# Jumping knowledge as one block: turned messages normed, weighed and summed in place in PSUM

## The chip, the cores and the metric

The kernel runs on one NeuronCore of a Trainium2 chip. The metric is the device time of one execution in microseconds, the median of several runs.

## The reference

The program is a chain of four graph networks over 50000 nodes with 128 features and 25000 edges, sorted by their end `dst`; each network's output is added to its input and the sum is layer-normed. The change is in the third network alone (jumping knowledge), which runs four layers:

```python
norm_src = rsqrt(max(deg_out, 1)); norm_dst = rsqrt(max(deg_in, 1))
for i in range(4):
    agg = segment_sum((h * norm_src)[src], dst, num_segments=n)
    h = relu((agg * norm_dst) @ Ws[i] + bs[i])
    mu, var = mean(h, axis=0), var(h, axis=0)
    h = relu((h - mu) * rsqrt(var + 1e-5) * gammas[i] + betas[i])
    xs.append(h)
out = relu(max(stack(xs), axis=0) @ lin1_w + lin1_b)
```

A node that no edge ends in has the same row in every layer, `relu(bs[i])` before the norm.

## The kernel before, in words

All sizes are fixed: the 25000 edges lie in 25088 slots, 49 groups (`EG`) of 512 (`GROUP`), each of four pieces (`SUB`) of 128. `K.goes_on` (a byte per slot) tells whether a slot has the same end as the one before it, `K.last_row` whether it is the last of its end, `K.l2_weight` holds each slot's weight, a number per partition. A layer's rows are stored to a table in HBM, `jk0` to `jk2`, one row per slot and one more row that all nodes without edges share; `idx_jk` points a slot at the row of its source, and at that shared row if the source is no edge's end. Layer 0 reads the table `x2` (in the trace `x`) instead.

`jk_start_block` makes the weights and the shared rows. Then `jk_layer_block` runs once for each layer, and each block opens and closes with a barrier of all engines. In a layer, each group goes through these steps:

- POOL (`pool_gather`, L570) issues four indirect DMAs, each of 128 rows, into `jk_layer_msg`, five groups deep (`DEEP`). It waits until the buffer's user of five groups ago is done.
- In layers 1 to 3 DVE puts the norm of the layer before on the rows: it multiplies by `W.jk_scale_row` (L1908) and adds `W.jk_shift_row` (L1910), into `jk_layer_ready`. These are rows, spread over the partitions at a layer's end by two matmuls.
- ACT weighs (`scalar_weigh`, L1023, four instructions a group, with Relu in layers 1 to 3), PE turns the rows into columns in PSUM (`tensor_sum`, L1057), DVE sums along the slots with a scan (L1079, PSUM to SBUF).
- PE multiplies by the layer's matrix (`make`, L696), ACT adds the bias and takes Relu (`keep`, L1886), SP stores the result turned (`jk_t`), DVE takes the two moments over the last slots of each end (`count`, L1916 and L1919, both with an accumulator).
- In layers 0 to 2 PE turns it back (`turn`, L687), ACT copies it out (L1891), and SP stores it to the table (L1850) from which the next layer gathers.

`run_groups(engine, n, stages)` writes an engine's program: it goes through the steps and calls each stage for the group that its lag says, so the order on an engine is fixed in the code. `g.lag(k)` is the group k before, and `wait_for` waits until that group has passed the named point. At a layer's end DVE works out scale and shift from the moments, with a root on ACT, and the barrier follows.

## Time and profile before

| | us |
|---|---|
| time, median of 3 runs (6713.34 to 6717.9) | 6714.33 |
| span of the profiled execution | 7555.6 |
| the four layers' gathers, first to last of each | 4005.5 to 4297.5, 4327.3 to 4623.0, 4653.4 to 4951, 4980 to 5268.5 |

No time beside its span is given for the profiled execution. It is 841 us or 12.5% above the median, so lengths in the trace are those of a slower execution than the timed ones. A busy time is that of an engine's own work; idle time before a group of instructions is named with what ended it, and "issue" is the engine's own pause between two instructions.

### The profile page before, as it was taken

What the parts mean: (1) busy time and instruction counts of PE and PEld (TensorE: products, weight loads), DVE (VectorE), ACT (ScalarE), POOL (GpSimd) and SP (SyncE); (2) the same over time, 40 slices, a digit from 0 to 9 for tenths busy, and PEclk for the clock granted to TensorE, in tenths of its full rate; (3) what the DMA queues carried; (4) which work ended last, traced back from release to release, by engine and by line L of the source; (5) the groups of instructions that cost most, each with busy time, mean ns of one, the idle gap of its engine ahead of it and who ended that gap; (6) DMA issues with size and microseconds to landing.
All of it is one profiled execution on the core that took longest, in us unless ns stands there. A gap on an engine that the chain in (4) does not pass through costs nothing. (4 is left out here: it accounts for less than half of the span.)

```text
span 7555.6 us, 86623 instructions
## 1 busy us (share of the span) xinstructions
PE 4855.1 (64%) x23532; PEld 3254.8 (43%) x23532; DVE 4654.8 (62%) x13695; ACT 3050.2 (40%) x6979; POOL 3999.0 (53%) x3991
## 2 busy tenths in 40 slices
PE   6888888779978625686233443434899995579211
PEld 4666665445558403575222222211555553346111
DVE  4777666223358627668674455656899995644444
ACT  3555554443334103344343333333677773245000
POOL 4565553544435466556555565656333334654766
PEclk9999999889989755796555666766899997789555
DMA  6988665776768423696343475754677675565232
GB/s 143 226 240 231 209 206 188 215 215 226 243 201 245 121 45 92 187 257 185 109 122 103 124 118 110 128 96 88 234 248 256 244 251 156 173 183 177 84 88 73
DMA packets 1104141, 1292.14 MB, mean 171 GB/s; under 512 B 133903, under 2 KB 815679, under 8 KB 1097390
## 3 DMA queue, kind: packets, MB, share of 16 engines
q1 hardware_dynamic: 973518, 1032.63, 43.5%
q0 software_dynamic: 130144, 253.97, 16.5%
q8 instruction: 197, 3.23, 0.2%
q14 instruction: 282, 2.31, 0.1%
HBM read 607.93 MB, written 682.10 MB: 171 GB/s over the span
## 5 line engine op out<-in xcount | busy, mean ns | idle before, releaser
L570 POOL DMA_INDIRECT jk_layer_msg<-jk,idx_jk x588 | 593.7, 1010 | 376.5 <-issue 173.4
L1057 PE MATMUL jk_layer_sum_ps<-ident,jk_layer_weighted 128*128 128x128 f32 x784 | 178.9, 369 | 733.6 <-ACT jk_layer_weighted L1023 382.1
L2084 POOL TENSOR_TENSOR rows_moved<-rows_x_in,w_lonely_row 128x512 f32<-128x512 f32 x98 | 124.6, 1272 | 677.3 <-DVE rows_x L671 640.9
L1057 PEld LDWEIGHTS jk_layer_sum_ps<-ident,jk_layer_weighted 128*128 128x128 f32 x784 | 114.6, 183 | 844.8 <-ACT jk_layer_weighted L1023 431.5
L1079 DVE TENSOR_TENSOR_SCAN jk_layer_sum_t<-goes_on,jk_layer_sum_t,jk_layer_sum_ps 128x512 f32<-128x512 uint8 x196 | 250.1, 1276 | 346.3 <-DMA sage_nodes_x_in<-in_x 288.0
L1886 ACT ACTIVATE jk_layer_h_t<-jk_layer_h_ps,w_jk_b 128x512 f32<-128x512 f32 x196 | 134.7, 687 | 631.8 <-DMA gat_own<-yv 337.9
L696 PE MATMUL sage_nodes_h_ps<-sage_nodes_h_t,w_ws 128*128 128x512 f32 x784 | 353.6, 594 | 0.0
L1198 DVE COPY sage_h<-sage_turn 128x512 f32<-128x512 f32 x98 | 67.8, 692 | 456.7 <-PE sage_turn L687 348.3
L894 ACT ACTIVATE sage_nodes_h_t<-sage_nodes_h_ps,w_b_c 128x512 f32<-128x512 f32 x392 | 248.9, 688 | 239.8 <-PE sage_nodes_h_ps L696 114.8
L696 PE MATMUL sage_h_ps<-sage_sum_t,w_wn 128*128 128x512 f32 x588 | 296.7, 614 | 59.0 <-issue 58.8
L2283 PE MATMUL gcn_end_sum_ps<-ident,gcn_end_rows 128*128 128x128 f32 x196 | 54.7, 434 | 426.9 <-DVE gcn_end_rows L2276 215.4
L570 POOL DMA_INDIRECT sage_msg<-h,idx x196 | 185.7, 948 | 247.4 <-ACT sage_weighted L1023 166.4
L570 POOL DMA_INDIRECT sage_end_msg<-h,idx x196 | 193.8, 989 | 224.4 <-ACT sage_end_weighted L1023 113.5
L696 PE MATMUL jk_layer_h_ps<-jk_layer_sum_t,w_jk_w 128*128 128x512 f32 x392 | 297.0, 852 | 0.6 <-DVE jk_layer_sum_t L1079 0.4
L687 PE MATMUL sage_nodes_ring<-ident,sage_nodes_h_t 128*128 128x128 f32 x1568 | 221.9, 288 | 106.7 <-issue 98.7
L696 PE MATMUL sage_h_ps<-sage_own_t,w_ws 128*128 128x512 f32 x588 | 290.0, 602 | 0.0
L1627 POOL DMA_INDIRECT second_msg<-u,idx_y x196 | 185.4, 946 | 182.4 <-PE second_x_ps L679 108.3
L1137 POOL DMA_INDIRECT place_of_src<-place,src_node x196 | 185.5, 947 | 167.7 <-issue 67.6
L1179 ACT ACTIVATE sage_h_t<-sage_h_ps,w_b_c 128x512 f32<-128x512 f32 x196 | 124.3, 685 | 357.9 <-PE sage_h_ps L696 296.6
L570 POOL DMA_INDIRECT jk_layer_msg<-x,idx x196 | 194.4, 992 | 139.2 <-issue 57.7
L570 POOL DMA_INDIRECT gcn_msg<-r,idx x196 | 191.9, 979 | 142.4 <-DVE gcn_rows L2276 65.8
L557 POOL DMA_INDIRECT src_count<-counts,src_node x196 | 192.3, 981 | 138.3 <-SPq L135 93.6
(454 smaller groups left out, 16299.8 us busy)
## 6 DMA issues: line engine op xcount, KB each, us to landing
h<-sage_nodes_h SPq DMA_DIRECT2D x196, 512.0 KB
h_t<-sage_h_t SPq DMA_DIRECT2D x98, 512.0 KB
h<-sage_h SPq DMA_DIRECT2D x98, 512.0 KB
jk_t<-jk_layer_h_t SPq DMA_DIRECT2D x196, 256.0 KB
rows_layers<-jk_t SPq DMA_DIRECT2D x49, 1024.0 KB, 5.9
r<-rows_h SPq DMA_DIRECT2D x98, 512.0 KB
second_x_in<-u SPq DMA_DIRECT2D x147, 260.0 KB
jk<-jk_layer_h SPq DMA_DIRECT2D x147, 256.0 KB
```

The costliest lines, as they stand in the source:

```text
L557: pool.indirect_dma_start(out=self.K.src_count[:, t:t + 1], out_offset=None, in_=self.table, in_offset=bass.IndirectOffsetOnAxis(ap=self.K ...
L570: pool.indirect_dma_start(out=into[:, g.number % depth, s, :], out_offset=None, in_=table, in_offset=bass.IndirectOffsetOnAxis(ap=index_ti ...
L687: mm = pe.transpose(ps[:, n, c * P:(c + 1) * P], feats[:, c, s * P:(s + 1) * P], ident[:])
L696: mm = pe.matmul(ps[:, c, :], w[:, k, c * P:(c + 1) * P], x[:, k, :], start=n == 0, stop=n == len(terms) - 1)
L894: ins = act.activation(tile[:, g.b, c, :], ps[:, c, :], ACT.Relu, bias=bias[:, c:c + 1])
L1057: mm = pe.transpose(ps[:, c, at_s], self.weighted[:, g.b, s, c * P:(c + 1) * P], self.K.ident[:])
L1079: dve.tensor_tensor_scan(self.sum_t[:, g.b, c, :], self.K.goes_on[:, cols(g, GROUP)], self.ps[g.b][:, c, :], self.sum_t[:, 1 - g.b, c, GRO ...
L1137: pool.indirect_dma_start(out=K.place[:, t:t + 1], out_offset=None, in_=tables["place"], in_offset=bass.IndirectOffsetOnAxis(ap=K.src_node ...
L1179: ins = act.activation(h_t[:, g.b, c, :], h_ps[:, c, :], ACT.Relu, bias=bias[:, c:c + 1])
L1627: pool.indirect_dma_start(out=msg[:, r % 4, s, :], out_offset=None, in_=tables["u"], in_offset=bass.IndirectOffsetOnAxis(ap=K.idx_y[:, col ...
L1886: act.activation(h_t[:, g.b, 0, :], h_ps[g.b][:, 0, :], ACT.Relu, bias=W.jk_b[:, i:i + 1]).then_inc(kept.sem, 1)
L2084: pool.tensor_tensor(moved[:, g.b], x_in[:, g.number % 3], to_subs(W.lonely_row), ALU.add).then_inc(lonely_added.sem, 1)
```

## The change

One block, `jk_block`, takes the place of the start block and the four layer blocks. Its jobs are numbered through (`job(i, g)`), so no barrier stands between layers: POOL waits for the last three stores of the layer before, and ACT for the new scale and shift. In a group:

- the gathers stay as they are, eight groups deep instead of five, and a buffer is free once PE has turned it;
- PE turns the rows as they came (L679 into `msg_ps`, three PSUM banks); in layers 1 to 3 one ACT instruction per group puts scale, shift and Relu on the turned bank (`norm`), where scale and shift are numbers per partition;
- DVE multiplies the bank by the weights (`weigh`), scans it in place (`carry`), and multiplies by `K.last_row` into `sum_t` (`ends`), so slots that are no end give the constant `relu(b)` after the matrix;
- the weights vary along the bank now, so they are stored once as a row (`l2_row`) and SP loads 512 of them per group for all 128 partitions (`load_weight`);
- ACT takes the two moments itself (`accum_out` of `keep`, and a second pass with Square), and DVE's `count` is gone. The row forms of scale and shift, and their matmuls, are gone too.

```diff
-def jk_start_block(nc, K, W, tables):
-def jk_layer_block(nc, i, K, W, tables):
...
+def jk_block(nc, K, W, tables):
+    ph = Phase(nc, "jk", LAYERS * EG)
+    deep = 8
+    msg = ph.sb("msg", [P, deep, SUB, D])
+    weight = ph.sb("weight", [P, 3, GROUP])
...
+    @block.sync
...
+        for i in layers:
+            def load_weight(g):
+                j = job(i, g)
+                wait_for(sp, weighed, j.lag(3))
+                sp.dma_start(weight[:, j.number % 3, :], tables["l2_row"][cols(g, GROUP)].partition_broadcast(P)).then_inc(weight_in.of(j), 16)
...
+            run_groups(sp, EG, [(load_weight, -2), (store_t, 2)] + ([] if i == LAST else [(store, 3)]))
...
+    @block.gpsimd
+    def _(pool):
+        for i in layers:
+            if i == 1:
+                pool.wait_ge(const_stored, 16 * LAST)
+            if i:
+                for k in range(3):
+                    wait_for(pool, h_stored, Group(i * EG - 1 - k))
+            table, index = (tables["x2"], K.idx) if i == 0 else (tables[f"jk{i - 1}"], K.idx_jk)
+            for g in range(EG):
+                j = Group(i * EG + g)
+                wait_for(pool, msg_turned, j.lag(deep))
...
+    @block.tensor
...
+            def turn_messages(g):
+                j = job(i, g)
+                wait_for(pe, arrived, j)
+                wait_for(pe, masked, j.lag(3))
+                wait_for(pe, summed, j.lag(2))
+                turn_rows(pe, msg_ps[j.number % 3], msg[:, j.number % deep], K.ident).then_inc(msg_turned.sem, 1)
...
+            run_groups(pe, EG, [(make, 2)] + ([] if i == LAST else [(turn, 3)]) + [(turn_messages, 0)])
...
+    @block.scalar
...
+            def norm(g):
...
+                act.activation(bank[:], bank[:], ACT.Relu, bias=W.jk_shift[:, i - 1:i], scale=W.jk_scale[:, i - 1:i]).then_inc(normed.sem, 1)
+
+            def keep(g):
...
+                wait_for(act, counted, j.lag(1))
+                act.activation(h_t[:, j.number % 3, 0, :], h_ps[j.b][:], ACT.Relu, bias=W.jk_b[:, i:i + 1],
+                               accum_out=h_sum[:, cols(g, 1)]).then_inc(kept.sem, 1)
+                wait_for(act, kept, j)
+                act.activation(square[:], h_t[:, j.number % 3, 0, :], ACT.Square, bias=minus_const[:, i:i + 1],
+                               accum_out=square_sum[:, cols(g, 1)]).then_inc(counted.sem, 1)
...
+            if i:
+                act.wait_ge(scale_ready, i)
+            run_groups(act, EG, [(keep, 2)] + ([] if i == LAST else [(out, 3)]) + ([(norm, 0)] if i else []))
...
+    @block.vector
...
+                dve.tensor_tensor(bank[:], bank[:], weight[:, j.number % 3, :], ALU.mult).then_inc(weighed.sem, 1)
...
+                dve.tensor_tensor_scan(bank[:], K.goes_on[:, cols(g, GROUP)], bank[:], before, ALU.mult, ALU.add).then_inc(summed.sem, 1)
...
+                dve.tensor_tensor(sum_t[:, j.number % 3, 0, :], msg_ps[j.number % 3][:], K.last_row[:, cols(g, GROUP)], ALU.mult).then_inc(masked.sem, 1)
+            run_groups(dve, EG, [(weigh, 0), (carry, 0), (ends, 0)])
```

What this does to POOL's program, from the start block to the block after the layers. Before, where L135 and L136 are a block's end and its barrier:

```order
L136 ISA x2
L1856 UNCONDITIONAL_BRANCH
L570 DMA jk_layer_msg<-x,idx 128x128 x196
L135 UNCONDITIONAL_BRANCH
L136 ISA
L1856 UNCONDITIONAL_BRANCH
L570 DMA jk_layer_msg<-jk,idx_jk 128x128 x196
L135 UNCONDITIONAL_BRANCH
L136 ISA
L1856 UNCONDITIONAL_BRANCH
L570 DMA jk_layer_msg<-jk,idx_jk 128x128 x196
L135 UNCONDITIONAL_BRANCH
```

And in the changed kernel:

```order
L570 DMA mean_msg<-yv,idx_y 128x128 x196
L135 UNCONDITIONAL_BRANCH
L136 ISA
L1841 UNCONDITIONAL_BRANCH
L1854 DMA jk_msg<-x,idx 128x128 x196
L1854 DMA jk_msg<-jk,idx_jk 128x128 x588
L135 UNCONDITIONAL_BRANCH
```

The 784 gathers now stand behind one another, 196 of layer 0 and 588 of layers 1 to 3, with waits but no barrier between them.

DVE's program in the middle of layer 1, one group (the scan is printed as SCALAR_TENSOR_TENSOR). Before:

```order
L1916 SCALAR_TENSOR_TENSOR jk_layer_off,jk_layer_off_sum<-jk_layer_h_t,w_jk_const,last_row 128x512
L1919 SCALAR_TENSOR_TENSOR jk_layer_square,jk_layer_square_sum<-jk_layer_off 128x512
L1908 TENSOR_TENSOR jk_layer_ready<-jk_layer_msg,w_jk_scale_row 128x512
L1910 TENSOR_TENSOR jk_layer_ready<-jk_layer_ready,w_jk_shift_row 128x512
L1079 SCALAR_TENSOR_TENSOR jk_layer_sum_t<-goes_on,jk_layer_sum_t,jk_layer_sum_ps 128x512
```

In the changed kernel, the last group of layer 0 and the start of the moments behind it:

```order
L1944 TENSOR_TENSOR jk_msg_ps<-jk_msg_ps,jk_weight 128x512
L1954 SCALAR_TENSOR_TENSOR jk_msg_ps<-goes_on,jk_msg_ps 128x512
L1961 TENSOR_TENSOR jk_sum_t<-jk_msg_ps,last_row 128x512
L1964 TENSOR_REDUCE jk_small<-jk_h_sum 128x1
L1965 TENSOR_REDUCE jk_small<-jk_square_sum 128x1
```

Five instructions with two accumulators have become three, of which each reads the PSUM bank and one SBUF tile; layer 0 had three and keeps three.

## Rows read from the trace of the kernel before

**Rows 1.** The page: the span.
```profile
span 7555.6 us, 86623 instructions
```

**Rows 2.** The four layers from first to last gather. Columns: busy us (count) of PE, PEld, DVE, ACT, POOL; granted clock; DMA share; GB/s.
```profile
4005.50:4297.50 292.00, 131.93 (x436) 77.24 (x437) 118.35 (x216) 103.16 (x264) 193.71 (x196) 0.65 0.46 119
4327.30:4623.00 295.70, 123.09 (x426) 72.46 (x427) 170.49 (x301) 101.34 (x259) 196.00 (x195) 0.66 0.68 115
4653.40:4951.00 297.60, 121.56 (x435) 71.80 (x436) 174.12 (x307) 103.33 (x264) 197.05 (x196) 0.68 0.69 116
4980.00:5268.50 288.50, 102.48 (x265) 45.81 (x266) 173.12 (x305) 82.97 (x223) 199.15 (x196) 0.60 0.48 83
```

**Rows 3.** Groups of POOL over the whole trace: busy us, mean ns, idle before.
```profile
L570 POOL DMA_INDIRECT jk_layer_msg<-jk,idx_jk x588 | 593.7, 1010 | 376.5 <-issue 173.4 <-DVE jk_layer_ready L1908 114.5 <-POOLq L137 88.6
...
L570 POOL DMA_INDIRECT jk_layer_msg<-x,idx x196 | 194.4, 992 | 139.2 <-issue 57.7 <-POOLq L137 40.9 <-ACT jk_layer_weighted L1023 40.5
...
L570 POOL DMA_INDIRECT sage_msg<-h,idx x196 | 185.7, 948 | 247.4 <-ACT sage_weighted L1023 166.4 <-issue 46.9 <-POOLq L137 34.2
L1137 POOL DMA_INDIRECT place_of_src<-place,src_node x196 | 185.5, 947 | 167.7 <-issue 67.6 <-DVE sage_sum_t L1079 63.0 <-POOLq L137 37.1
```

**Rows 4.** The timeline where layers 0 and 1 start and behind layer 3: start, length, engine.
```profile
4001.19 0.26 DVE L1799 TENSOR_SCALAR l_weight<-src_count 128x196 f32<-128x196 f32 x1 [3.45 <-PEq L137]
...
4005.52 0.95 POOL L570 DMA_INDIRECT jk_layer_msg<-x,idx  x1 [40.89 <-POOLq L137]
...
4009.27 0.95 POOL L570 DMA_INDIRECT jk_layer_msg<-x,idx  x1 [0.31 <-issue]
...
4011.74 1.28 ACT L1023 ACTIVATE jk_layer_weighted<-jk_layer_msg,l_weight 128x128 f32<-128x128 f32 x4 [9.89 <-DMA jk_layer_msg<-x,idx]
...
4297.27 0.95 POOL L570 DMA_INDIRECT jk_layer_msg<-x,idx  x1 [0.30 <-issue]
4327.35 0.95 POOL L570 DMA_INDIRECT jk_layer_msg<-jk,idx_jk  x1 [29.12 <-POOLq L137]
...
5294.81 0.16 DVE L1958 TENSOR_TENSOR lonely_each<-w_jk_const,w_jk_scale 128x4 f32<-128x4 f32 x1 [1.42 <-PEq L137]
```

**Rows 5.** Groups of DVE by form, whole trace.
```profile
L1079 DVE TENSOR_TENSOR_SCAN jk_layer_sum_t<-goes_on,jk_layer_sum_t,jk_layer_sum_ps 128x512 f32<-128x512 uint8 x196 | 250.1, 1276 | 346.3 <-DMA sage_nodes_x_in<-in_x 288.0 <-PE jk_layer_sum_ps L1057 31.9 <-issue 16.4
...
L1919 DVE SCALAR_TENSOR_TENSOR jk_layer_square<-jk_layer_off 128x512 f32<-128x512 f32 x196 | 135.7, 692 | 6.8
...
L1685 DVE TENSOR_TENSOR second_node_v<-second_node_ps,w_gat_b 128x512 f32<-128x512 f32 x98 | 67.5, 689 | 99.5 <-DMA kept<-u,idx 61.1 <-PE second_wide_ps L705 18.7 <-PE second_node_ps L705 14.7
```

**Rows 6.** Groups of ACT by form, whole trace.
```profile
L1660 ACT ACTIVATE second_x_t<-second_x_ps,w_ln_shift,w_ln_scale 128x512 f32<-128x512 f32 x196 | 150.9, 778 | 217.5 <-PE second_x_ps L679 149.6 <-DMA kept<-u,idx 38.0 <-issue 20.5
```

**Rows 7.** The timeline of layer 0 around 4115 us, where PE has finished.
```profile
4114.22 1.12 PE L1057 MATMUL jk_layer_sum_ps<-ident,jk_layer_weighted 128*128 128x128 f32 x4 [5.70 <-issue]
4115.13 1.91 PE L696 MATMUL jk_layer_h_ps<-jk_layer_sum_t,w_jk_w 128*128 128x512 f32 x2
...
4122.22 1.28 DVE L1079 TENSOR_TENSOR_SCAN jk_layer_sum_t<-goes_on,jk_layer_sum_t,jk_layer_sum_ps 128x512 f32<-128x512 uint8 x1 [7.69 <-DMA sage_nodes_x_in<-in_x]
4122.26 0.69 ACT L1886 ACTIVATE jk_layer_h_t<-jk_layer_h_ps,w_jk_b 128x512 f32<-128x512 f32 x1 [2.33 <-DMA gat_own<-yv]
```

**Rows 8.** The timeline at the end of layer 0.
```profile
4313.71 1.27 ACT L1023 ACTIVATE jk_layer_weighted<-jk_layer_msg,l_weight 128x128 f32<-128x128 f32 x4
...
4318.22 0.69 ACT L1886 ACTIVATE jk_layer_h_t<-jk_layer_h_ps,w_jk_b 128x512 f32<-128x512 f32 x1 [0.47 <-PE jk_layer_h_ps L696]
...
4319.41 2.03 SPq L1850 DMA_DIRECT2D jk<-jk_layer_h  x2
```

**Rows 9.** DMA queues by packets, MB, share of 16 engines: 4340 to 4640, then 4985 to 5280 us.
```profile
q0 software_dynamic: 5994, 12.28, 45.3%
q1 hardware_dynamic: 30448, 23.99, 23.9%
...
q1 hardware_dynamic: 6624, 12.06, 10.8%
```

More of the change, by code:

```diff
@@ L1791, in _, with out @@
     @block.scalar
     def _(act):
-        act.wait_ge(to_root, 1)
-        act.activation(K.l2_weight[:], K.l2_weight[:], ACT.Sqrt).then_inc(root, 1)
+        act.wait_ge(l2_capped, 1)
+        act.activation(K.l2_weight[:], K.l2_weight[:], ACT.Sqrt).then_inc(l2_root, 1)
+        for i in layers:
+            def norm(g):
+                j = job(i, g)
+                wait_for(act, msg_turned, j)
+                bank = msg_ps[j.number % 3]
+                act.activation(bank[:], bank[:], ACT.Relu, bias=W.jk_shift[:, i - 1:i], scale=W.jk_scale[:, i - 1:i]).then_inc(normed.sem, 1)
+            def keep(g):
+                j = job(i, g)
+                wait_for(act, made, j)
+                wait_for(act, ht_stored, j.lag(3))
+                if i < LAST:
+                    wait_for(act, turned, j.lag(3))
+                wait_for(act, counted, j.lag(1))
[4 more added lines that the diff above has]
+                               accum_out=square_sum[:, cols(g, 1)]).then_inc(counted.sem, 1)
+            def out(g):
+                j = job(i, g)
+                wait_for(act, turned, j)
+                wait_for(act, h_stored, j.lag(3))
+                act.copy(h[:, j.number % 3], lanes(rows_ps[j.b], D)).then_inc(out_done.sem, 1)
+            if i:
+                act.wait_ge(scale_ready, i)
+            run_groups(act, EG, [(keep, 2)] + ([] if i == LAST else [(out, 3)]) + ([(norm, 0)] if i else []))
+            act.wait_ge(to_root, i + 1)
+            act.activation(small[:, 3:4], small[:, 1:2], ACT.Sqrt, bias=W.eps[:]).then_inc(rooted, 1)
@@ L1798, in _ @@
         link = linker(dve, chain)
-        dve.tensor_scalar(K.l2_weight[:], K.src_count[:], 1.0, None, ALU.max).then_inc(to_root, 1)
-        dve.tensor_scalar(W.jk_const[:], W.jk_b[:], 0.0, None, ALU.max).then_inc(made, 1)
-        dve.wait_ge(turned, 1)
-        dve.tensor_copy(row[:], row_ps[:]).then_inc(copied, 1)
-        dve.wait_ge(root, 1)
-        link(dve.reciprocal(K.l2_weight[:], K.l2_weight[:]))
-        link(dve.tensor_tensor(K.l2_weight[:], K.l2_weight[:], K.norm_dst[:], ALU.mult))
@@ new lines, in _ @@
+        dve.tensor_scalar(K.l2_weight[:], K.src_count[:], 1.0, None, ALU.max).then_inc(l2_capped, 1)
+        dve.tensor_scalar(W.jk_const[:], W.jk_b[:], 0.0, None, ALU.max).then_inc(const_made, 1)
+        dve.wait_ge(const_made, 1)
+        link(dve.tensor_scalar(minus_const[:], W.jk_const[:], -1.0, None, ALU.mult))
+        dve.wait_ge(const_turned, 1)
+        dve.tensor_copy(const_row[:], start_ps[0:LAYERS, 2, :]).then_inc(const_copied, 1)
+        dve.wait_ge(l2_root, 1)
+        link(dve.reciprocal(K.l2_weight[:], K.l2_weight[:]))
@@ L1947, in lonely_block, with spread_column @@
+    ph.close()
+def spread_column(dve, pe_ready, diag, ident, column):
+    dve.tensor_scalar(diag[:], ident[:], column, None, ALU.mult).then_inc(pe_ready, 1)
 def lonely_block(nc, K, W):
@@ L2495, in resnorm_gnn @@
     tables["jk_t"] = nc.dram_tensor("jk_t", [EG, P, LAYERS, GROUP], F32, kind="Internal").ap()
+    tables["l2_row"] = dram("l2_row", SLOTS, 0)
     for i in range(LAYERS):
@@ L2528, in resnorm_gnn @@
         mean_block(nc, A, K, W, tables)
-        jk_start_block(nc, K, W, tables)
-        for i in range(LAYERS):
-            jk_layer_block(nc, i, K, W, tables)
+        jk_block(nc, K, W, tables)
         ends.close()
```

230 lines of the change are left out of this document (103 added, 127 removed).

## The prediction

> **What bounds the kernel now.** I read the page first: the profiled execution spans 7555.6 us [rows 1]; the median of the timed runs is 6714.33 us. The change touches one stretch only, from the start block's first instruction at 4001.19 us to the first one behind the layers at 5294.81 [rows 4]: 1293.6 us, 17% of the span.
>
> Then the windows, one a layer [rows 2]. POOL is the busiest engine in each (194 to 199 us of 288 to 298), and behind each of its gathers lies a pause that the groups name as issue: 57.7 us over 196 gathers and 173.4 over 588 [rows 3], 0.295 us each. So a gather costs POOL 0.992 + 0.295 = 1.29 us in layer 0 and 1.010 + 0.295 = 1.305 us in the others: 5.15 and 5.22 us a group, 1020 us for all 784. No other engine has as much: DVE is busy 118 us in layer 0 and 170 to 174 after, PE 102 to 132, ACT 83 to 103, the DMA engines 0.46 to 0.69 of the time [rows 2].
>
> What POOL waits for beyond its own pace is 40.5 us (for the weighing in layer 0) and 114.5 us (for L1908 in the others) [rows 3], 155 us in all, and the pauses between layers. The timeline shows where the 155 us come from. PE's rows say that the layer's matmul that began at 4115.13 took 1.91 us; the scan and the `keep` that wait for PE start at 4122.22 and 4122.26, together and 5 us late [rows 7]. Such hold-ups come back all through the layers, one in five to eight groups. Two results of PE that were ready at different times and are let go in the same instant look like news of PE's work held back, not like slow work. The profiled execution is 841 us longer than a timed one, and I take most of these hold-ups to belong to profiling. With them gone the stretch is paced by POOL alone: 1020 us of gathers, 4.3 of start, and four drains.
>
> **The change part by part.** *A cheaper gather.* The gathers stay, 784 of them. But their price differs with what DVE does beside them: 0.992 and 1.010 us in the layers, 0.948 and 0.947 where a phase's DVE only scans and copies out of PSUM [rows 3]. In the layers DVE squares SBUF tiles (L1919) and adds a row to one (L1910); afterwards each of its three instructions reads one PSUM operand. I price the new gather at 0.947: 196 x 0.045 + 588 x 0.063 = 8.8 + 37.0 = **45.8 us less**. Bounds: nothing, if the difference has another cause, and 46, since no row of gathers is cheaper. The Trainium skill (GPSIMD Engine Reference, Specifications) says that GpSimd shares its SBUF interfaces with VectorE and that instructions with two SBUF inputs contend. By that rule L1908 and L1916 would contend too, and all of the excess would go; these rows do not tell the four lines apart.
>
> *The start.* POOL's first gather is issued at 4005.52, 4.3 us behind the start block's first instruction [rows 4], since the block and its barrier stand ahead of it. Now it is first in its block: **4.3 us less**. The first weighing stands 6.2 us behind the first gather (4005.52 to 4011.74 [rows 4]). The new weight row needs a root, two turns, a store and a load, of which I take each transfer at the 2.5 us of a gather's landing and the rest at 4 us: 9 us. So the first group is 3 us late, and that is hidden, since POOL may run eight groups ahead, 40 us.
>
> *The boundaries.* The gap between the layers' gathers is 29 to 30 us in the trace [rows 2]. Held news is in it: the gather issued at 4297.27 should be weighed 2.5 us after its issue (4009.27 to 4011.74 [rows 4]) and was weighed at 4313.71 [rows 8]. Without it the old drain is 2.5 + (4327.35 - 4313.71) = 16.1 us, and 17.5 in layers 1 and 2, with the two DVE passes at 0.69. The new one: arrival 2.5, turning 1.1 [rows 7], weigh 0.69, scan 1.27, ends 0.69 [rows 5], matmul 1.91 [rows 7], hand-offs at an estimated 0.4, from `keep` to the last store's issue 3.2 (4318.22 to 4321.44 [rows 8]), the square in between 0.8, landing 2.5 as of a gather, less 0.5 because PE often runs the matmul at the higher clock: 14.6, and with the norm at 0.78 [rows 6] 15.4. Three boundaries: 1.5 + 2.1 + 2.1 = **5.7 us less**. The moments, the scale and the shift are no longer on this path: they are ready some 4 us after the last `keep`, while the next layer's first group needs the store, 5 us of gathers and 2.5 of arrival. The last layer's end keeps its moments and its barrier; I take 0.5 us.
>
> *ACT and DVE.* ACT was busy 101 us in layer 1, 2.1 us a group [rows 2]. It gets norm 0.78 [rows 6], keep 0.69 [rows 8], square at the norm's 0.78, copy at keep's 0.69, and two accumulator outputs, which no row of ACT shows: between nothing and a whole pass more each. That is 2.9 to 4.3 us, all below POOL's 4.97; I take 3.2, since the accumulators give one number. DVE has 0.69 + 1.27 + 0.69 = 2.65 us. The longest loop, over two groups: make(g-2) 1.9, turn 1.1, turning 1.1 [rows 7], norm 0.8, weigh 0.7, scan 1.3, ends 0.7, hand-offs 0.5, is 8.1 us, 4.05 a group. All this is covered by POOL; if POOL's pace were below 4.05 us, the loop would show. Behind the new wait of PE for a group's arrival stand make(g-1) and with it ACT's keep(g-1); both have a group's time to spare, and the eight buffers make up for a late one.
>
> *The weight loads.* 196 loads of 128 x 2 KB, no row shows one in this stretch. The nearest is the store of `jk_t`, as many packets of the same size: layer 3 stores hardly anything else, 10.8% of 295 us for 12.06 MB, 46 stores, so 0.69 us a store over all 16 engines [rows 9]. In layer 1 (2 is alike) the queues take 45.3 + 23.9 = 69% of 300 us for 12.28 MB of gathers, 47 groups [rows 9], 4.4 us a group; with the load 5.1 us, against POOL's 4.97. So they would be about full there. Part of a packet's time is waiting among others, so I cost it at nothing, with the queue's slack in layers 0 and 3 certain and in 1 and 2 thin. The Trainium skill (DMA: Bandwidth & Descriptors, SWDGE vs HWDGE vs iDMA) says each DMA engine serves the software and the hardware queues in turn; by that, more packets on SP's queue lengthen the gathers' landings, which speaks against the change in layers 1 and 2. The eight buffers hide a longer landing, not a full queue.
>
> Sum: -45.8 - 4.3 - 5.7 - 0.5 = **-56 us**. In the profiled execution's time that is 1293 to some 1237 of the stretch, and more if the deeper buffer takes up hold-ups. The terms are engine times and not shares, so I set them against the median unscaled: 6714 - 56 = **6658 us**.
>
> **The rivals.** *The hold-ups are real in timed runs too.* For: they are in the trace, and so are POOL's 155 us of waits [rows 3]. Against: the 841 us. Then PE's hold-ups set the pace and not POOL, and the cheaper gather buys nothing. At worst the change takes none of the waits away and only the start and the boundaries are left, 10.5 us; at best eight buffers and fewer signals of PE (three a group, six before) bring POOL to its own pace, and 155 + 56 = 211 us go. In the middle, 110 us: 6604.
>
> *The DMA engines become the bound.* For: 5.1 us a group by the sum above. Sources without edges all read one shared row, and the gathers' packets take 45.3% there; if 128 partitions reading one 2 KB row suffer likewise, the load costs twice 0.69, and layers 1 and 2 run at 5.8 us a group. That is 98 x 0.58 = 57 us more than before there, in place of the 25 us less: -56 + 25 + 57 = +26, 6740, slower. At 5.5 us a group it is -4, 6710, no change. The point from which it decides is 5.54 us, 0.32 above the old pace. Against: part of the gathers' time is queueing, and the old trace reaches this load only in short bursts.
>
> *The change doesn't do what it says for POOL*: gathers stay at 1.0 us. Then 10.5 us less: 6704, no change that can be told.
>
> **How the numbers follow.** A measurement of this kernel tells 0.2%, 13 us, from none. My forecast 0.58 (own range 6635 to 6690, nearly all of it faster); real hold-ups 0.14 (faster); the price of a gather unchanged 0.09 (same); DMA-bound 0.19, of which 0.12 slower and 0.07 same. Faster 0.70, same 0.18, slower 0.12. The range leaves out the far end of the real hold-ups and the worst of the DMA case, 2 in 10 at most with what I have not thought of: 6575 to 6735.
>
> **What would show it.** POOL's group of gathers at 0.95 us and not 1.0; gaps between layers well under 29 us; the first gather right at the block's start; no DVE line with two SBUF inputs; POOL's own waits for `msg_turned` near nothing. The DMA share of layers 1 and 2 near 0.8 if I am right, at 0.95 with PE waiting for arrivals if the rival is. I am wrong if the gathers' price does not move, or if POOL's pace in timed runs is so much better than in the trace that the loop or the DMA engines set the time.

## The result, and the profile after

The changed kernel takes 6764.51 us (median of 4 runs, 6762.32 to 6771.9), the kernel before 6713.84 us beside it: ratio 1.0076, 95% interval 1.0063 to 1.0088. It is 51 us slower, where I forecast 56 us less.

This time the profiled execution is as long as the timed ones, 6764.0 us. POOL's groups of the jumping-knowledge gathers over the whole trace (busy us, mean ns, idle before and what ended it) answer to [rows 3]:

```profile
span 6764.0 us, 85845 instructions
L1854 POOL DMA_INDIRECT jk_msg<-jk,idx_jk x588 | 554.7, 943 | 348.2 <-issue 171.3 <-DMA jk<-jk_h 97.8 <-PE jk_msg_ps L679 79.1
L1854 POOL DMA_INDIRECT jk_msg<-x,idx x196 | 184.9, 944 | 80.2 <-issue 58.8 <-POOLq L137 20.8 <-PE jk_msg_ps L679 0.6
```

The gather is at the price I forecast, 0.943 us. But POOL waits 79.1 us for `msg_turned` and 97.8 us for the stores between the layers. The windows of the four layers (columns as in [rows 2]) and the DMA queues of layer 1 (packets, MB, share of 16 engines):

```profile
3461.90:3705.30 243.40, 136.25 (x473) 81.75 (x472) 129.39 (x147) 94.65 (x231) 183.99 (x195) 0.74 0.75 203
3720.20:4038.20 318.00, 140.44 (x490) 82.06 (x490) 133.24 (x158) 136.61 (x295) 184.91 (x196) 0.68 0.92 162
4038.20:4357.20 319.00, 139.99 (x490) 82.27 (x490) 133.03 (x158) 136.16 (x295) 184.92 (x196) 0.70 0.91 162
4357.20:4608.30 251.10, 109.90 (x266) 49.87 (x266) 116.57 (x131) 97.48 (x212) 183.98 (x196) 0.63 0.91 139
...
q0 software_dynamic: 6272, 12.86, 53.1%
q1 hardware_dynamic: 39920, 38.43, 38.2%
```

The first and the last window are a layer from first to last gather, the middle two run from a layer's first gather to the next one's, so they hold the drain. Layer 0 runs at POOL's own pace: 243.4 us for 195 gathers, 1.248 each. Layers 1 and 2 move fewer bytes a second (162 GB/s against 203) with a higher DMA share (0.92 against 0.75), and no compute engine is busy for more than 59% of them. The waits of layer 1 (total us, times, longest), and the timeline in one place of it:

```profile
PE jk_h_ps L1877 <- DVE jk_sum_t L1961: 121.5, 33, 13.3
DVE jk_msg_ps L1944 <- ACT jk_msg_ps L1895: 91.6, 34, 11.0
DVE jk_msg_ps L1944 <- DMA jk_weight<-l_row: 83.0, 10, 15.4
...
ACT jk_h L1914 <- DMA jk<-jk_h: 53.5, 16, 8.4
PE jk_msg_ps L679 <- DMA jk_msg<-jk,idx_jk: 52.1, 16, 11.7
POOL jk_msg L1854 <- DMA jk<-jk_h: 51.8, 2, 37.8
...
POOL jk_msg L1854 <- PE jk_msg_ps L679: 39.2, 11, 12.4
```
```profile
3850.64 9.48 SPq L1826 DMA_DIRECT2D jk_weight<-l_row  x1
...
3857.30 0.94 POOL L1854 DMA_INDIRECT jk_msg<-jk,idx_jk  x1 [0.30 <-issue]
...
3863.73 0.70 DVE L1944 TENSOR_TENSOR jk_msg_ps<-jk_msg_ps,jk_weight 128x512 f32<-128x512 f32 x1 [15.15 <-DMA jk_weight<-l_row]
...
3866.61 2.07 PE L1877 MATMUL jk_h_ps<-jk_sum_t,w_jk_w 128*128 128x512 f32 x2 [13.32 <-DVE jk_sum_t L1961]
...
3869.33 1.06 PE L679 MATMUL jk_msg_ps<-ident,jk_msg 128*128 128x128 f32 x4
...
3870.66 0.94 POOL L1854 DMA_INDIRECT jk_msg<-jk,idx_jk  x1 [12.41 <-PE jk_msg_ps L679]
```

Four of these waits are for transfers themselves: DVE waits for a weight load, PE for gathered rows, ACT for a store to leave its buffer, POOL for the last stores of a layer. Others pass such a wait on, as the place shown does. A weight load took SP 9.48 us to issue, where the fastest of the layer took 0.32. DVE stood 15.15 us for its weights, PE's matmul 13.32 us for DVE, and the turning of the next messages comes behind that matmul in PE's program. POOL, which had run its eight groups ahead, stood 12.41 us for the turning. Here it was the weights that came late, not the rows.

### The profile page after: what moved, and what is told of

It reads as the page before. It is cut to its first block and busy times, and to the rows that moved or that the text cites. A ratio compares the mean times of both kernels' runs of the same rounds, so it can differ in the third digit from the quotient of the medians.

```text
span 6764.0 us, 85845 instructions
## 1 busy us (share of the span) xinstructions
PE 4739.2 (70%) x23518; PEld 3202.3 (47%) x23522; DVE 4451.0 (66%) x12999; ACT 3093.9 (46%) x6930; POOL 3952.1 (58%) x3991
## 5 line engine op out<-in xcount | busy, mean ns | idle before, releaser
L1854 POOL DMA_INDIRECT jk_msg<-jk,idx_jk x588 | 554.7, 943 | 348.2 <-issue 171.3
L1877 PE MATMUL jk_h_ps<-jk_sum_t,w_jk_w 128*128 128x512 f32 x392 | 312.0, 890 | 323.4 <-DVE jk_sum_t L1961 323.3
L1944 DVE TENSOR_TENSOR jk_msg_ps<-jk_msg_ps,jk_weight 128x512 f32<-128x512 f32 x196 | 137.1, 699 | 596.7 <-ACT jk_msg_ps L1895 260.5
L679 PE MATMUL jk_msg_ps<-ident,jk_msg 128*128 128x128 f32 x784 | 172.9, 361 | 292.7 <-DMA jk_msg<-jk,idx_jk 185.2
L1904 ACT ACTIVATE jk_h_t<-jk_h_ps,w_jk_b 128x512 f32<-128x512 f32 x196 | 134.7, 687 | 431.5 <-PE jk_h_ps L1877 263.0
L679 PEld LDWEIGHTS jk_msg_ps<-ident,jk_msg 128*128 128x128 f32 x784 | 124.7, 187 | 376.0 <-DMA jk_msg<-jk,idx_jk 237.7
L570 POOL DMA_INDIRECT sage_nodes_fetched<-in_x,src_x x196 | 206.9, 1055 | 104.8 <-issue 49.1
L1954 DVE TENSOR_TENSOR_SCAN jk_msg_ps<-goes_on,jk_msg_ps 128x512 f32<-128x512 uint8 x196 | 253.3, 1292 | 21.2 <-DVE jk_msg_ps L1944 1.4
L599 POOL DMA_INDIRECT kept<-u,idx x196 | 194.8, 994 | 112.7 <-issue 59.4
L671 DVE TENSOR_SCALAR rows_z<-rows_y,rows_norm_moments,rows_norm_root 128x128 f32<-128x128 f32 x392 | 255.3, 710 | 3.6
L570 POOL DMA_INDIRECT gcn_end_msg<-y,idx x196 | 188.2, 960 | 110.0 <-issue 59.4
```

The lines of the kernel that those rows point to most:

```text
L570: pool.indirect_dma_start(out=into[:, g.number % depth, s, :], out_offset=None, in_=table, in_offset=bass.IndirectOffsetOnAxis(ap=index_ti ...
L599: pool.indirect_dma_start(out=kept[:, t, :], out_offset=None, in_=table, in_offset=bass.IndirectOffsetOnAxis(ap=K.idx[:, t:t + 1], axis=0) ...
L671: ins = dve.tensor_scalar(out[:, g.number % depth, s, :], rows[:, g.b, s, :], self.moments[:, g.b, s, 0:1], self.root[:, g.b, s, 0:1], ALU ...
L679: mm = pe.transpose(ps[:, s * P:(s + 1) * P], rows[:, s, :], ident[:])
L1854: pool.indirect_dma_start(out=msg[:, j.number % deep, s, :], out_offset=None, in_=table, in_offset=bass.IndirectOffsetOnAxis(ap=index[:, g ...
L1877: pe.matmul(h_ps[j.b][:], W.jk_w[:, i, :], sum_t[:, j.number % 3, 0, :], start=True, stop=True).then_inc(made.sem, 1)
```

## The experiments

All ratios are to the kernel before, run on the same chip; two variants that ran on different chips are compared by these ratios. POOL's waits for a buffer and the gaps between layers are read from each trace. The mean time of a gather's packet is worked out from the queue's row: of q0's packets half carry 4 bytes and the others 4096 (12.86 MB in 3136), that is 16 to a gather, eight rows of 512 bytes each. So for layer 1 of the changed kernel it is 0.531 x 318.0 x 16 / 3136 = 0.86 us, with the small ones counted as nothing.

**The kernel before, profiled again** (unchanged; 6729.24 us). 

> The kernel before, unchanged, for a second profile, since the one shown spans 841 us more than a timed run. If the hold-ups of PE's news belong to that one execution, this span is near 6714 us, POOL's waits inside the four layers are near nothing, the layers from first to last gather take 196 x 1.25 to 1.3 = 245 to 256 us each, and the gaps between them 16 to 20 us. If they are real in every execution, the layers take 287 to 297 us again with 155 us of waits. The price of a gather beside the squaring DVE should be 0.99 to 1.01 us either way, if DVE's two SBUF operands cause it.

Its trace spans 6727.4 us and is not stretched. Windows of the four layers (the middle two with their drains), POOL's groups, and q0 in layer 1:

```profile
3473.50:3727.60 254.10, 139.56 (x465) 81.10 (x466) 127.49 (x232) 113.58 (x283) 194.69 (x196) 0.70 0.56 143
3747.50:4036.00 288.50, 153.16 (x494) 88.74 (x494) 195.77 (x358) 119.07 (x295) 198.65 (x197) 0.64 0.85 134
4036.00:4326.00 290.00, 149.09 (x494) 86.24 (x494) 196.11 (x358) 119.56 (x295) 197.70 (x197) 0.71 0.88 133
4326.00:4580.00 254.00, 117.66 (x280) 51.79 (x280) 182.82 (x323) 90.24 (x235) 194.60 (x195) 0.62 0.57 97
...
L570 POOL DMA_INDIRECT jk_layer_msg<-jk,idx_jk x588 | 591.9, 1007 | 260.5 <-issue 176.4 <-POOLq L137 78.9 <-DVE jk_layer_ready L1908 5.3
L570 POOL DMA_INDIRECT jk_layer_msg<-x,idx x196 | 195.6, 998 | 83.9 <-issue 59.4 <-POOLq L137 24.5
...
q0 software_dynamic: 6272, 12.86, 58.1%
```

Two things follow. POOL's wait of 114.5 us for L1908 [rows 3] is 5.3 us here: the hold-ups were the profiling's, as I had taken them. And the DMA share of layers 1 and 2 is 0.85 and 0.88, drains included, not 0.68: the stretched trace, which had added waits for POOL, had also hidden how full the DMA engines are. From first to last gather, as [rows 2] has it, layer 1 has 0.88. The shorter layer accounts for only about half of the step: 0.68 x 295.7 / 260.1 is 0.77. For the rest the gathers' packets took longer, 0.86 us each over layer 1's window here, against 0.73 by [rows 9] (0.453 x 300 x 16 / 2997). Against the changed kernel the time went here (us; layers from first to last gather):

| | before | changed | difference | predicted |
|---|---|---|---|---|
| ahead of the first gather | 24.5 | 20.8 | -3.7 | -4.3 |
| layer 0 | 254.1 | 243.4 | -10.7 | -8.8 |
| gap to layer 1 | 19.9 | 14.9 | -5.0 | -1.5 |
| layer 1 | 260.1 | 279.3 | +19.2 | -12.3 |
| gap to layer 2 | 28.3 | 38.7 | +10.4 | -2.1 |
| layer 2 | 256.2 | 272.0 | +15.8 | -12.3 |
| gap to layer 3 | 33.9 | 47.0 | +13.1 | -2.1 |
| layer 3 | 254.0 | 251.1 | -2.9 | -12.3 |
| behind the last gather | 17.2 | 30.8 | +13.6 | -0.5 |
| sum | | | +49.8 | -56 |

The stretch is 49.8 us longer; the two spans differ by 36.6, since they come from two chips and the rest of the program was 13 us shorter in the changed kernel's trace. Up to the start of layer 1 the change gives 19.4 us where 14.6 were predicted. From then on all is longer, and the old kernel's gaps behind layers 1 and 2 were already 8 and 14 us longer than the one behind layer 0.

**Without the weight loads.** The change with loads for the first three groups alone; the other 193 groups are weighed with stale weights.

```diff
             def load_weight(g):
                 j = job(i, g)
-                wait_for(sp, weighed, j.lag(3))
+                if j.number >= 3:
+                    return
...
-                wait_for(dve, weight_in, j)
+                wait_for(dve, weight_in, Group(j.number % 3))
```

> The changed kernel with weight loads for its first three groups only; all later groups are weighed with what then lies in the three buffers, so the weights of 193 groups are wrong. Nothing else differs. Theory A (the DMA engines are full in layers 1 to 3 and the weight loads fill them): the loads' 0.7 to 0.8 us a group go, the DMA share falls from 0.94 to about 0.85 at a shorter layer, POOL's waits (36, 29 and 8 us) and the long gaps between layers (38 and 46 us) shrink to some 16, and the time falls to 6640 to 6680, near what was forecast. Theory B (the new loop through PE, ACT and DVE sets the pace): no change, 6755 to 6775.

6706.63 us, ratio 0.9967 [0.9958, 0.9977]: 73 us less than the changed kernel by the ratios. So the loads, which I had costed at nothing, cost more than the whole difference. But without them it is only 22 us faster than before, not 56, and above the 6640 to 6680 us that I had expected. POOL's waits fall to 24.9 us, and the gaps behind layers 1 and 2 stay long:

```profile
L1855 POOL DMA_INDIRECT jk_msg<-jk,idx_jk x588 | 554.8, 943 | 297.8 <-issue 174.7 <-DMA jk<-jk_h 98.3 <-PE jk_msg_ps L679 24.9
...
q0 software_dynamic: 6272, 12.86, 59.2%
```

The second row is q0 in layer 1 (3724.7 to 4027.4): 0.91 us a packet. The loads did not make a gather's packet longer (0.86 with them); they took engine time of their own, and DVE's waits for them, 83.0 us in layer 1, are gone.

**The kernel before with the loads.** 196 loads of the same shape into a spare tile that no engine reads. SP alone waits for them, before it reuses the tile's two buffers and at a layer's end.

```diff
+        def load_extra(g):
+            wait_for(sp, extra_in, g.lag(2))
+            wait_for(sp, sums.summed, g.lag(3))
+            sp.dma_start(extra[:, g.b, :], tables["x_own"].rearrange("n d -> (n d)")[cols(g, GROUP)].partition_broadcast(P)).then_inc(extra_in.of(g), 16)
-        run_groups(sp, EG, [(store_t, 2)] + ([] if last else [(store, 3)]))
+        run_groups(sp, EG, [(load_extra, -2), (store_t, 2)] + ([] if last else [(store, 3)]))
         wait_for_all(sp, ht_stored)
+        wait_for_all(sp, extra_in)
```

> The kernel before, with 196 more loads of one 2 KB row for 128 partitions into a scratch tile that nobody reads, one a group, paced by PE's sum; the output is the reference's. Theory A: the loads fill the DMA engines here too, so the old kernel becomes slower by 60 to 120 us (6775 to 6835) and its messages arrive late in layers 1 and 2. Theory B: the loads cost nothing, 6705 to 6725.

6779.25 us, ratio 1.0077 [1.006, 1.0094]: 52 us. The loads by themselves, with nobody waiting for them to compute, cost the old kernel 52 us. So their transfers alone account for most of the 73 us that they cost the changed kernel. Whether the other 21 are DVE's wait for its weights or the deeper run-ahead, no run takes apart. That 52 is also what the whole change cost is a coincidence.

**Distinct rows.** The change, but layers 1 to 3 gather from `x2` with `K.idx` as layer 0 does, so no row is shared by the sources without edges; the rows of layers 1 to 3 are the wrong ones.

```diff
-            table, index = (tables["x2"], K.idx) if i == 0 else (tables[f"jk{i - 1}"], K.idx_jk)
+            table, index = (tables["x2"], K.idx)
```

> The changed kernel, but all layers gather the rows of the table of layer 0, by its own index, so no shared row is read again and again; layers 1 to 3 then work on the wrong rows. Weight loads and stores stay. Theory A with the shared row as the costly half of a gather: a gather's packets take 350 ns as in layer 0 and not 840, layers 1 to 3 run at POOL's pace with gaps of 16 us, 6640 to 6680. If the shared row costs nothing and the bytes alone count, the time stays at 6750 to 6770.

6631.23 us, ratio 0.9862 [0.9846, 0.9879]: 93 us less than before, with all loads in place. Layer 1's window and its queues, from first to last gather:

```profile
3731.50:3974.90 243.40, 132.95 (x466) 78.37 (x467) 126.05 (x141) 128.81 (x277) 183.98 (x195) 0.78 0.73 201
...
q1 hardware_dynamic: 36772, 36.15, 46.6%
q0 software_dynamic: 6190, 12.71, 26.1%
```

Same bytes, same packets, and layer 1 runs at POOL's pace. A gather's packet takes 0.261 x 243.4 x 16 / 3095 = 0.33 us instead of 0.86. But this kernel changes the table too, so it doesn't say yet that the shared row is the cause.

**128 copies of the shared row, in the changed kernel.** The gather of partition p reads copy p.

```diff
-        dve.tensor_scalar(K.idx_jk[:], where[:], float(SLOTS), None, ALU.min)
+        link(dve.tensor_copy(far[:], K.slot_no[:, 0:1]))
+        link(dve.tensor_scalar(far[:], far[:], float(SLOTS), None, ALU.add))
+        dve.tensor_scalar(K.idx_jk[:], where[:], far[:, 0:1], None, ALU.min)
...
-            sp.dma_start(tables[f"jk{i}"][SLOTS:SLOTS + 1], const_row[i:i + 1, :]).then_inc(const_stored, 16)
+            sp.dma_start(tables[f"jk{i}"][SLOTS:SLOTS + P].rearrange("(a n) d -> a n d", a=1), const_row[i:i + 1, :].unsqueeze(1).broadcast_to([1, P, D])).then_inc(const_stored, 16)
```

> The changed kernel, but the row that all nodes without edges share is stored 128 times in each table, and the gather of partition p reads copy p; same bytes, same number of packets, and the weight loads stay. Theory A (layers 1 and 2 are paced by the DMA engines because more than half of the gathered rows are one and the same row of HBM, whose packets take near 0.9 us instead of 0.35): the packets of layers 1 to 3 take what those of layer 0 do, POOL runs at its own pace of 243.4 us a layer, the gaps between layers are 14 to 16 us, and the time is that of the run with distinct rows, 0.985 to 0.989 of the kernel before (6630 to 6655 us). Theory B (the bytes of gathers, stores and loads together fill the DMA engines, whatever row they come from; the run with distinct rows was fast for another reason, for example because its table was x2): near the changed kernel, 1.005 to 1.009.

6632.88 us, ratio 0.986 [0.984, 0.988]: 94 us less than before and, by the ratios, 145 less than the changed kernel. Windows of the four layers from first to last gather, POOL's group, and q0 in layer 1:

```profile
3473.80:3717.30 243.50, 137.35 (x473) 83.45 (x472) 129.30 (x147) 95.07 (x231) 184.09 (x195) 0.74 0.76 204
3733.20:3976.70 243.50, 134.46 (x466) 78.64 (x467) 126.06 (x141) 128.45 (x277) 184.09 (x195) 0.77 0.71 202
3990.80:4234.30 243.50, 133.38 (x464) 78.94 (x465) 126.04 (x141) 128.33 (x276) 184.08 (x196) 0.75 0.70 202
4249.10:4492.60 243.50, 130.15 (x286) 54.42 (x286) 126.44 (x142) 108.48 (x232) 184.12 (x195) 0.61 0.56 154
...
L1857 POOL DMA_INDIRECT jk_msg<-jk,idx_jk x588 | 555.1, 944 | 220.2 <-issue 176.1 <-DMA jk<-jk_h 42.0 <-PE jk_msg_ps L682 2.1
...
q0 software_dynamic: 6190, 12.71, 23.4%
```

All four layers take the same 243.5 us, POOL's wait for a buffer is 2.1 us in place of 79.1, and the three gaps are 16, 14 and 15 us. The shared row is the cause.

**The same copies in the kernel before.** The same edit of `places_block` and of the rows' store.

> The kernel before with the same 128 copies of the shared row. Theory A: the old layers 1 and 2 were held up by the same packets, though less: their gathers go from 260 and 256 to 254 us, and the gaps behind layers 1 and 2 from 28 and 34 to some 18 us, so 30 us less, 0.994 to 0.997 of the kernel before; the gather itself stays at 1.00 us. The change made on top of it would then be worth some 50 us, near the 56 that the prediction counted. Theory B: no difference, 0.999 to 1.001.

6707.78 us, ratio 0.9971 [0.9961, 0.998]: 20 us less than before, 10 less than I expected.

```profile
3749.40:4007.30 257.90, 137.72 (x460) 80.11 (x460) 183.54 (x324) 111.01 (x279) 198.46 (x196) 0.71 0.52 140
...
L570 POOL DMA_INDIRECT jk_layer_msg<-jk,idx_jk x588 | 597.1, 1016 | 234.4 <-issue 178.2 <-POOLq L137 56.1
L570 POOL DMA_INDIRECT jk_layer_msg<-x,idx x196 | 196.7, 1003 | 91.9 <-issue 59.4 <-POOLq L137 32.5
```

The three gaps' wait is 56.1 us, where it was 78.9; but the wait ahead of layer 0 is 32.5 us, where it was 24.5, since the start block must store 384 rows before its barrier, and the gathers cost 1.016 us, where they had cost 1.007. With the row out of the way the change itself is worth 1.1% (0.986 against 0.9971), 75 us, of which 8 are that store. By the traces: 53.6 us in the layers, 14.2 in the gaps, 11.1 at the start (8 of them the store), 2 at the end.

**Five group buffers.** The change with `deep = 5`.

> The changed kernel with five group buffers for the gathers instead of eight, as before the change. Theory C (running further ahead makes more gathers stand in the DMA queues at once, so that each packet and each landing takes longer, and this is part of the loss): 10 to 25 us faster than the changed kernel, 1.003 to 1.006 of the kernel before, and the landings of a layer's last group shorter. Rival: the queue is full either way and depth only moves where POOL waits: 1.006 to 1.010, the layers' periods unchanged at 318 and 319 us; or slower still, if eight buffers hid late landings.

6749.7 us, ratio 1.0035 [1.0024, 1.0045]: the interval does not touch that of the change, and five buffers are 28 us better by the ratios, 26 by the traces. Layer 1 and layer 2 up to the next layer's first gather:

```profile
3733.60:4039.20 305.60, 141.41 (x490) 83.37 (x490) 132.88 (x158) 136.05 (x295) 185.06 (x197) 0.71 0.92 168
4039.20:4351.80 312.60, 142.19 (x490) 83.00 (x490) 133.21 (x158) 136.23 (x295) 185.00 (x197) 0.71 0.90 165
...
q0 software_dynamic: 6272, 12.86, 52.3%
```

The packet takes 0.82 us instead of 0.86; times 196 (3136 packets over 16 engines) that is 9 of layer 1's 12.4 us. So running further ahead costs, where the queue is full: POOL can have more rows in it, and each packet takes longer. Why more gathers in flight make a packet longer, no run here shows.

**Both: no loads, five buffers.** The two edits above together.

> The changed kernel with both: weight loads for the first three groups only (the weights of the others are wrong), and five group buffers instead of eight. If the two costs add up (64 us of the jumping-knowledge stretch for the loads, 26 for the depth), the stretch is 1117 - 26 = 1091 us against 1131 of the kernel before, and the time 0.993 to 0.995. If depth only costs because the loads stand in the same queues, five buffers without loads change nothing: 0.996 to 0.998, as without loads alone. The period of layer 1 is then 302 us as with eight buffers, and else near 285.

6691.16 us, ratio 0.9937 [0.9924, 0.9951], some 42 us less than before. Layer 1 takes 290.5 us to the next layer's first gather. The ratio lies where my first reading had it. But by the traces the four layers with their gaps and ends are only 14 us shorter than with eight buffers and no loads, where adding up asked for 26, and layer 1 lies between the two readings. So depth costs without the loads too. It costs less than with them by the traces (14 against 26 us); by the ratios, 20 against 28 us, that is within the intervals.

**Another source for the weights.** The 196 loads read a 2 KB row of its own for each partition; all weights are wrong.

```diff
-                sp.dma_start(weight[:, j.number % 3, :], tables["l2_row"][cols(g, GROUP)].partition_broadcast(P)).then_inc(weight_in.of(j), 16)
+                sp.dma_start(weight[:, j.number % 3, :], at(tables["h1_t"], g)[:, 0, :]).then_inc(weight_in.of(j), 16)
```

> The changed kernel, but the 196 weight loads read 128 rows of 2 KB from another table, a row of its own for each partition, in place of one row read 128 times; bytes and packets the same, the weights wrong in every group. If the loads cost what they cost because 128 packets read one row: back to the run without loads, 0.996 to 0.998 of the kernel before. If they cost by their bytes and packets: like the changed kernel, 1.006 to 1.009. I expect the second, since the median packet of these loads took 84 ns.

6779.01 us, ratio 1.0073 [1.0053, 1.0093], like the changed kernel. The broadcast of one 2 KB row isn't what makes the loads dear, so the point of my rival by which "128 partitions reading one 2 KB row suffer likewise" is refuted.

**How many copies, and where.** The gathers of layers 1, 2 and 3 read 2, 8 and 32 of the stored copies, copy p modulo that number.

```diff
+        for i, n in enumerate((2, 8, 32)):
+            link(dve.tensor_scalar(low[:], K.slot_no[:, 0:1], n - 1, None, ALU.bitwise_and))
+            link(dve.tensor_copy(few[:], low[:]))
+            link(dve.tensor_scalar(few[:], few[:], float(SLOTS), None, ALU.add))
+            link(dve.tensor_scalar(K.idx_few[i][:], where[:], few[:, 0:1], None, ALU.min))
```

> The changed kernel with the 128 copies of the shared row stored, of which the gathers read 2 in layer 1, 8 in layer 2 and 32 in layer 3 (copy p modulo that number). Correct output. Theory A, by packets: with one copy a gather's packet takes some 850 ns, with 128 copies 256 to 290. If what matters is how many reads fall on one row, 2 copies halve the excess (near 570 ns), 8 leave an eighth of it (350) and 32 nothing. Then layer 1 is still somewhat held up or just free (2 x 0.55 of the excess puts its DMA work near 75% of POOL's pace), and layers 2 and 3 run at 243.5 us. Rival: one row is slow for its place in memory and not for being shared, then 2 copies next to each other are as slow as one, and layer 1 keeps some 30 us of waits.

One run, 6628.22 us (before on the same chip: 6734.29). Layer 1, with two copies, and its q0:

```profile
3722.00:3965.80 243.80, 140.45 (x465) 80.17 (x466) 126.14 (x141) 128.74 (x277) 184.38 (x195) 0.74 0.72 202
...
q0 software_dynamic: 6200, 12.73, 25.5%
```

Two copies do all that 128 do: 0.32 us a packet, where halving the excess asked for 0.57. Layers 2 and 3, with 8 and 32 copies, take 243.9 us each too. So the number of reads that fall on a row is not what counts. The next run takes the same two copies, but partitions 0 to 63 read one and 64 to 127 the other (layer 2), and one copy alone in two places of the longer table (layers 1 and 3):

```diff
-        for i, n in enumerate((2, 8, 32)):
-            link(dve.tensor_scalar(low[:], K.slot_no[:, 0:1], n - 1, None, ALU.bitwise_and))
+        for i, (mask, first) in enumerate(((0, 0), (64, 0), (0, 64))):
+            link(dve.tensor_scalar(low[:], K.slot_no[:, 0:1], mask, None, ALU.bitwise_and))
...
-            link(dve.tensor_scalar(few[:], few[:], float(SLOTS), None, ALU.add))
+            link(dve.tensor_scalar(few[:], few[:], float(SLOTS + first), None, ALU.add))
```

> The changed kernel with the 128 copies stored in tables of 128 more rows, of which the gathers read: in layer 1 the first copy alone, in layer 2 two copies (partitions 0 to 63 the first, 64 to 127 the 65th), in layer 3 the 65th copy alone. Correct output. Since 2 copies in turn cured layer 1 as fully as 128, I see three readings. D, the same row read back to back by one DMA packet is slow (eight neighbouring partitions to a packet): all three layers have slow packets, near 850 ns, layer 2 too although it has two copies. E, the number of reads of one row is what counts, beyond a threshold: layer 2 near 300 ns, layers 1 and 3 near 850. F, it was the place or the length of the table, not the sharing: layer 1 or layer 3 near 300 ns with one copy. By D and E the layers come out at 260 to 280 us where the packets are slow, and the time between 6700 and 6765.

One run, 6780.36 us (before on the same chip: 6718.41), above the 6700 to 6765 that I expected. The three layers from first to last gather, and q0 in each:

```profile
3728.60:4000.50 271.90, 120.93 (x409) 71.25 (x410) 109.97 (x123) 111.41 (x238) 184.43 (x196) 0.70 0.94 159
4043.90:4312.10 268.20, 121.67 (x414) 71.78 (x414) 111.11 (x125) 112.03 (x241) 184.45 (x196) 0.70 0.95 161
4351.90:4598.40 246.50, 103.44 (x242) 45.79 (x242) 104.65 (x117) 89.46 (x192) 184.45 (x196) 0.62 0.88 134
...
q0 software_dynamic: 6044, 12.41, 58.0%
q0 software_dynamic: 6012, 12.34, 56.6%
q0 software_dynamic: 6090, 12.50, 64.8%
```

0.84, 0.81 and 0.84 us a packet: slow in all three. The place of the row and the length of the table don't matter, and two copies help only when neighbours read them in turn. That is reading D: the same row read several times on end, within the eight rows of a packet. That a packet's eight rows are those of neighbouring partitions isn't in the trace; it is inferred from these two runs. They differ in one thing more: the two copies lie one row apart where they helped and 64 rows apart where they didn't, and no run takes copies 64 rows apart in turn.

**Which operands raise the gather's price.** The changed kernel with 128 copies and a spare DVE instruction per group in layers 1 and 2.

```diff
+            def spare_work(g):
+                if i == 1:
+                    link(dve.tensor_tensor(spare[:, 2, :], spare[:, 0, :], spare[:, 1, :], ALU.add))
+                if i == 2:
+                    link(dve.tensor_scalar(spare[:, 2, :], spare[:, 0, :], 1.0, None, ALU.add))
```

> The changed kernel with 128 copies and one spare DVE instruction of 128 by 512 per group: in layer 1 one that adds two SBUF tiles, in layer 2 one that adds a constant to one SBUF tile, in layers 0 and 3 none. Output unchanged. If the gathers' price on GpSimd rises because DVE reads two SBUF tiles, the gathers of layer 1 take about 0.944 + 0.03 = 0.97 us on the mean, for one such instruction a group (three of them a group went with 1.007 us, two in layer 0 with 1.000), and those of layers 0, 2 and 3 stay at 0.943. If any SBUF work of DVE does it, layer 2 rises as well; if the price has another cause, neither does.

One run, 6632.23 us. POOL's gathers of layers 0, 1, 2 and 3, each layer's window by itself:

```profile
L1858 POOL DMA_INDIRECT jk_msg<-x,idx x196 | 184.9, 943 | 80.8 <-issue 56.1 <-POOLq L137 21.4 <-PE jk_msg_ps L682 3.4
L1858 POOL DMA_INDIRECT jk_msg<-jk,idx_jk x196 | 192.0, 980 | 74.9 <-issue 57.0 <-DMA jk<-jk_h 15.5 <-PE jk_msg_ps L682 2.4
L1858 POOL DMA_INDIRECT jk_msg<-jk,idx_jk x196 | 185.8, 948 | 73.1 <-issue 58.8 <-DMA jk<-jk_h 13.7 <-PE jk_msg_ps L682 0.6
L1858 POOL DMA_INDIRECT jk_msg<-jk,idx_jk x196 | 184.9, 943 | 72.9 <-issue 59.4 <-DMA jk<-jk_h 13.5
```

The sum of two SBUF tiles costs the four gathers of its group 4 x 37 = 148 ns on the mean, the one with a single SBUF input 4 x 5 = 20 ns, and POOL is 7 us longer in layer 1. The two also differ in length, 0.683 and 0.437 us, but by far less than in cost. A measurement agrees here with the Trainium skill (GPSIMD Engine Reference, Specifications), which has instructions with two SBUF inputs contend.

## Why the prediction was wrong

*What bounds the kernel now.* POOL's pace, as I had it, was right for layer 0, where the gathers run without a wait of POOL's own, and the hold-ups were profiling's. But in layers 1 and 2 it was right only just: unstretched, the DMA engines had 0.85 x 288.5 / 49 = 5.0 us of work a group, where I worked out 4.4, against a pace of 5.3. I threw out the stretched trace's waits and kept its DMA shares, which were too low for a run without the stretching.

*A cheaper gather: right, and its cause shown in kind.* 0.943 us in all four layers, where I priced 0.947, from 0.998 and 1.007. One spare instruction with two SBUF inputs brings back 37 ns. The old kernel had two such a group in layer 0 and four in the others, for 55 and 64 ns; what each of its lines costs was not measured. Where the DMA engines had room it was worth more than the 45.8 us counted: 53.6 us. In the changed kernel only layer 0's 10.7 came through.

*The start and the boundaries: right in mechanism, the second too small.* -3.7 us against -4.3. The gap between layers 0 and 1 shrank by 5.0 us where I had 1.5, and with the copies the three together by 14.2 where I had 5.7: the new drain was sized well (16, 14 and 15 us against 14.6 and 15.4), and the old one, without the held news, was some 19 to 21 us and not 16.1 and 17.5.

*ACT and DVE: covered, as said.* ACT took 136.61 us for layer 1, 2.8 a group; I had 3.2, and my upper bound of 4.3 should have been 4.4 by its own terms. The accumulator's cost, which no row showed, is an extra read of 193 ns in this group of ACT:

```profile
L1904 ACT ACTIVATION_READ_ACCUMULATOR jk_h_t<-jk_h_ps,w_jk_b 128x1 f32 x196 | 37.7, 193 | 0.0
```

*The weight loads: the step that failed.* What the prediction costed at nothing, because part of a packet's time is waiting among others, took 73 us by the ratios. The forecast is missed by 107 us, from 56 less to 51 more. Without the loads 34 of them are left, and without the eight buffers as well 14. With 128 copies of the shared row nothing is left of the miss: the changed kernel is then 94 us below the kernel before, loads and eight buffers included.

Two terms under it were off. The load took the hardware queue from 0.266 x 288.5 / 49 = 1.57 to 0.382 x 318.0 / 49 = 2.48 us a group, 0.91 and not 0.69. And the gathers took 0.581 x 288.5 / 49 = 3.4 us, not the 2.9 of [rows 9]. The sum is some 5.9 us a group (0.92 x 318 / 49 = 6.0 measured), past the 5.54 us from which, as I had worked out, this decides. The rival named the bound, the place and the point where it decides, and gave 6740 for 5.8 us a group; it had a chance of 0.19, and should have been the forecast. Its sign came true: a DMA share of 0.94 from first to last gather of layer 1, with PE waiting 52.1 us for rows. That its 5.8 lies so near 6.0 is in part luck, since it doubled the load for a broadcast that costs nothing extra and kept the gathers at 2.9. It still fell short of the time measured (6764.51); among what it left out are weights that come late and hold DVE and PE (83.0 us of waits in layer 1), the longer landing behind the last gather (+13.6 us in the table) and what the deeper buffers cost (26 us).

The rule of the Trainium skill that it was weighed with (DMA: Bandwidth & Descriptors, SWDGE vs HWDGE vs iDMA), each engine serving software and hardware queues in turn, would have pointed the right way. The traces agree in the sign of the time, but do not show the rows coming later: in layer 1 PE waited 52.1 us for rows with the loads and 64.9 without, and a packet took 0.86 us with them and 0.91 without. What came late were the weights, and POOL's wait rose from 24.9 to 79.1 us behind them.

*The eight buffers* were said to help against a longer landing and not against a full queue, which was right and too kind. With a full queue they cost 28 us.

*What stood in the rows.* [Rows 2] have layer 0 at 119 GB/s for a DMA share of 0.46 and layer 1 at 115 GB/s for 0.68. The same gathers moved no more bytes, and the DMA engines were busy half as long again (0.46 x 292.0 against 0.68 x 295.7). I saw the shared row and passed it on to a rival as a question about the loads; the gathers themselves were where it bit.

*Still open:* why the packets get longer with more gathers in flight, and why the change without loads needs 302.7 us for layer 1 where the old kernel needs 288.5 for the same bytes (with five buffers 290.5, so most of it is depth). From first to last gather it is the faster one, 256.9 us against 260.1; what it loses, it loses in the gap behind, 45.8 us against 28.3.

## What to carry to other kernels

Before adding transfers, or speeding up what issues them, set each stage's DMA share against its GB/s: a stage whose share is high at a low rate has slow packets, and its slack is what the unstretched trace shows, not the stretched one. If a profiled execution is much longer than the timed ones, its shares of a resource can be too low as its waits are too long: take a second profile before either is used. Where an index table clamps many entries to one row, store the row more than once and let neighbouring partitions read the copies in turn: here 128 copies turned a loss of 0.8% into a gain of 1.4%, and 2, 8 and 32 in the three layers were as fast.

## What the runs showed of the hardware

- In layers 1 and 2 a gather's packet of eight 512-byte rows took 0.27 to 0.33 us with distinct rows or copies read in turn, and 0.80 to 0.91 us when many neighbouring indices named the same row (0.72 in the stretched execution). The row's place in a table with room for 128 copies made no difference (0.84 and 0.84 us).
- 196 loads of one 2 KB row to 128 partitions, which no other engine waited for, cost the kernel before 52 us. A broadcast cost the same as 128 rows of their own (ratios 1.0076 and 1.0073).
- An indirect DMA's time on POOL rose from 0.943 to 0.980 us with one DVE instruction of two SBUF inputs beside four of them, and to 0.948 with one of a single SBUF input.
- With five group buffers instead of eight, layer 1's packets took 0.82 us and not 0.86, and the kernel was 28 us faster.
